# A hybrid model on one Trainium2 core: the first block's order of work laid out anew, four of its units' segments on GpSimd, and the first expert unit's gate and up inside it

## The chip, the cores and the metric

One core of a Trainium2 chip runs the whole kernel. The core has five engines that run in parallel, each with its own queue of instructions taken strictly in order: TensorE (matmul, PE in the profile), VectorE (DVE), ScalarE (ACT), GpSimd (POOL) and SyncE (SP, which here issues the DMAs). They wait for each other through semaphores. TensorE writes only to PSUM, eight banks of 128 x 512 f32; SBUF is the large on-chip memory. The metric is device time in microseconds, the median of several runs.

## The reference, cut to what matters

The input is x of 4 sequences x 512 tokens x 128 features in f32. Four layers follow, each added to its own input after a layer norm:

```python
x = x + attn_a(layernorm(x))   # rotary q, then a Mamba-2 style scan
x = x + ffn(layernorm(x))      # 8 experts, the best 2 per token, and a shared one
x = x + attn_b(layernorm(x))   # RWKV time mixing and channel mixing
x = x + ffn(layernorm(x))      # the same expert layer again
```

In attn_a, q is projected and rotated, normed (rmsnorm) and projected to z (256), xBC (512) and dt (4 heads). xBC passes a causal convolution of four taps and silu. dt = softplus. The scan runs in chunks: within a chunk y = (C B^T * L) (x dt), where L = exp of the segment sums of dt*A; between chunks a state of 128 x 64 per head is decayed and added to. y + D x is multiplied by silu(z), normed and projected by W_out to 128 features, and q is added.

In ffn each branch is (silu(x Wg) * (x Wu)) Wd with 256 hidden features; the result is weighted by the router.

## The kernel before, in words

The program has two blocks, `phase_mamba` (layer 1) and `phase_body` (layers 2 to 4). A block ends when all engines have reached its end; then the next begins. In both, every engine's order of work is written out by hand.

**First block.** A tile is 128 tokens; there are 16, four per sequence. The block first norms x (VectorE `statistics`, `normalise`), turns it (`turn_x`), projects q (`project_q`), multiplies by the rotary tables (`turn_q`, `add_q`), norms and turns again (`turn_h`), and projects: `project_in` for the convolution (16 banks of 512 columns; VectorE adds three taps each in `taps`, ScalarE does the first, `tap0`), `project_z` (L1060: one tile of 256 columns in one bank, ScalarE `z_silu`, 16 times) and `project_dt`. dt passes exp and ln on ScalarE (`dt_exp`, `dt_log`) and becomes adt in `finish_dt`; until then no segment can be made. `turn_tok` turns the convolved tokens back.

The scan then works in 16 units, each one tile of one sequence: units 0 to 7 belong to sequences 0 and 1, units 8 to 15 to sequences 2 and 3. Per unit n: ScalarE `segments` (L807) writes `seg_l[n % 2]` as four products of 128 x 128; TensorE `seg_sums` (L1097) sums them, ScalarE `seg_exp` takes the exponential; TensorE `products` makes C B^T, VectorE `masking` and `mixing` join the two; GpSimd `weigh_x`, `skip_x` and `decay_x` prepare x dt, D x and the weighted x; TensorE `within` and `carry` make y, `add_state` the state, VectorE `joining` and `new_state` read them; GpSimd `gating` multiplies by silu(z); then comes the way out: TensorE `turn_g`, ScalarE `copy_gT`, TensorE `project_out`, and VectorE `closing` adds q. All ways out use one bank, so `turn_g(n)` waits for `closing(n - 1)` (L1150). Beside it, `split_high` and `split_low` cut the nine branches' expert weights into two f16 halves each.

At the end of the block `tile_stats`, `tile_means` (L593) and GpSimd's `rsqrt_out` (L344) make the layer norm of the expert layer, the first half of the tiles and the second; `apply_norm`, `turn_first`, `copy_x`, `cast_x` and `split_x` prepare the first sequence's input to the experts (x_hi and x_lo).

**Second block.** 72 units, one branch of one sequence (slot q, branch e, u = 9q + e). Per unit and half: TensorE `gate_up` (L1533) makes gate and up, three f16 matmuls of 512 columns each; ScalarE `gate` takes silu; VectorE `hidden` multiplies; ScalarE `high` casts; GpSimd `low` makes the rest; two units later TensorE's `down` (L1550) follows. The router's `logits` stand beside unit 0, with the exponential in `route_exp` on ScalarE. `beside` places the work of layer 3 between units. The statistics of sequence 3 are made in slot 1 (`has_stats`, L1522); those of the first three sequences come from the first block.

## Time and profile before

| | |
|---|---|
| median of 3 runs | 508.76 us (507.75 to 509.42) |
| the profiled execution | 507.94 us, of which 505.6 us span |
| TensorE busy | 470.4 us, 93% of the span |
| VectorE, ScalarE, GpSimd busy | 391.0, 360.3 and 360.6 us |
| mean granted TensorE clock | 0.982 |
| first block | from 0 to about 133 us |

The page of the profile has these lines:

```profile
PE   3787999998599999999999999999999989999994
DVE  5897999777376687889888898888887868477664
ACT  1789999874375867976696958694886566868552
POOL 4564676788276658789879879888889586466652
PEclk9999899999599999999999999999999999999999
```

Each digit is the busy share of a fortieth of the span (12.6 us) in tenths, and PEclk is TensorE's granted clock in tenths of full speed. The eleventh slice, 126 to 139 us, is the end of the first block and the start of the second: all four engines have a low digit there, and the clock stands at 5. A granted clock of 1.00 is 2.4 GHz and 0.50 is 1.2 GHz. Busy time of matmuls overlaps from one to the next.

### The profile page before, as it was taken

Reading aid. Unit: us, or ns where it says so; the run is one execution under the profiler, and the core shown is the slowest. Engines: PE = TensorE matmul, PEld = TensorE weight load, DVE = VectorE, ACT = ScalarE, POOL = GpSimd, SP = SyncE. Lnnn points to the kernel's source line nnn. Section 1 sums busy time; section 2 is a strip of 40 time slices with the busy share of each in tenths; the row PEclk is TensorE's granted clock in tenths of the full one; section 3 lists DMA queues with packets and bytes.
Section 4 is the critical chain, followed back from the end, with each engine's and each line's share of the span. In section 5 each row is a group of like instructions: output and inputs, shape, how many; then the busy total and the mean of one; then the engine's idle time right before and its main releaser. Section 6 shows DMA issues by size and latency. Waiting matters only on the chain.

```text
span 505.6 us, 10587 instructions
## 1 busy us (share of the span) xinstructions
PE 470.4 (93%) x3662; PEld 322.8 (64%) x3662; DVE 391.0 (77%) x1051; ACT 360.3 (71%) x711; POOL 360.6 (71%) x445
## 2 busy tenths in 40 slices
PE   3787999998599999999999999999999989999994
PEld 2555788997256666665565765666566756666663
DVE  5897999777376687889888898888887868477664
ACT  1789999874375867976696958694886566868552
POOL 4564676788276658789879879888889586466652
PEclk9999899999599999999999999999999999999999
DMA  8102011000010000000000000000000000000000
GB/s 275 38 3 87 8 32 33 1 2 3 6 63 0 2 1 2 2 2 1 1 2 1 1 1 1 1 2 3 0 1 22 2 1 23 0 2 1 22 1 21
DMA packets 7012, 8.49 MB, mean 17 GB/s; under 512 B 560, under 2 KB 5168, under 8 KB 6960
## 3 DMA queue, kind: packets, MB, share of 16 engines
q1 hardware_dynamic: 6960, 7.83, 4.8%
q8 instruction: 29, 0.48, 0.4%
q14 instruction: 23, 0.19, 0.1%
HBM read 6.78 MB, written 1.05 MB: 15 GB/s over the span
## 4 chain that ended last, share of the span: by engine, by line
PE 55%; DVE 8%; POOL 5%; ACT 3%; issue 2%; DVEq 0%; POOLq 0%; ACTq 0%
PE bank L1544 9%; PE bank L1548 9%; PE bank L1545 9%; PE bank L1563 5%; PE bank L1565 5%; PE bank L1564 5%; PE bank L1680 3%; PE bank L1663 2%; PE bank L1606 2%; DVE x L1914 2%; PE bank L1607 2%; POOL b_hc L2195 1%; PE bank L1591 1%; PE bank L1570 1%; DVE b_hid L1898 1%
## 5 line engine op out<-in xcount | busy, mean ns | idle before, releaser
L2133 POOL TENSOR_TENSOR b_hid_lo<-b_hid,b_hid_hi 128x512 f16<-128x512 f32 x144 | 167.8, 1177 | 56.7 <-ACT b_hid_hi L1740 54.5
L1898 DVE SCALAR_TENSOR_TENSOR b_hid<-bank,b_silu 128x512 f32<-128x512 f32 x144 | 97.8, 688 | 62.0 <-ACT b_silu L1733 36.7
L1733 ACT ACTIVATE b_silu<-bank 128x512 f32<-128x512 f32 x144 | 85.9, 597 | 58.9 <-PE bank L1548 58.5
L1544 PE MATMUL bank<-x_hi,wsplit 128*128 128x512 f16 x288 | 110.2, 382 | 5.5 <-PEq L130 4.8
L1545 PE MATMUL bank<-x_hi,wsplit 128*128 128x512 f16 x288 | 110.2, 382 | 0.0
L1548 PE MATMUL bank<-x_lo,wsplit 128*128 128x512 f16 x288 | 110.2, 382 | 0.0
L1563 PE MATMUL bank<-wsplit,b_hid_hi 128*128 128x128 f16 x576 | 100.2, 219 | 4.3 <-DVE x L1914 2.6
L1740 ACT CAST b_hid_hi<-b_hid 128x512 f16<-128x512 f32 x144 | 88.2, 612 | 21.9 <-DVE b_hid L1898 21.7
L1565 PE MATMUL bank<-wsplit,b_hid_lo 128*128 128x128 f16 x576 | 100.2, 219 | 0.0
L1564 PE MATMUL bank<-wsplit,b_hid_hi 128*128 128x128 f16 x576 | 100.2, 219 | 0.0
L1914 DVE SCALAR_TENSOR_TENSOR x<-bank,b_w_branch,x 128x128 f32<-128x128 f32 x256 | 71.5, 342 | 16.1 <-PE bank L1565 16.0
L1563 PEld LDWEIGHTS bank<-wsplit,b_hid_hi 128*128 128x128 f16 x576 | 56.6, 98 | 15.1 <-POOL b_hid_lo L2133 5.6
L1564 PEld LDWEIGHTS bank<-wsplit,b_hid_hi 128*128 128x128 f16 x576 | 56.3, 98 | 7.1 <-issue 1.3
L1565 PEld LDWEIGHTS bank<-wsplit,b_hid_lo 128*128 128x128 f16 x576 | 56.4, 98 | 0.0
L1548 PEld LDWEIGHTS bank<-x_lo,wsplit 128*128 128x128 f16 x288 | 28.4, 99 | 34.7 <-issue 1.1
L1544 PEld LDWEIGHTS bank<-x_hi,wsplit 128*128 128x128 f16 x288 | 28.4, 99 | 33.9 <-issue 8.8
L1545 PEld LDWEIGHTS bank<-x_hi,wsplit 128*128 128x128 f16 x288 | 28.3, 98 | 27.6 <-issue 4.8
L502 DVE SCALAR_TENSOR_TENSOR xbc<-bank,cols,xbc 128x511 f32<-128x511 f32 (+2 forms) x48 | 35.6, 747 | 2.0 <-ACT xbc L775 0.7
L812 ACT ACTIVATE seg_l<-after,adt 128x128 f32<-128x128 f32 x64 | 20.4, 401 | 0.0
L1106 PE MATMUL bank<-causal,seg_l 128*128 128x128 f32 x128 | 17.9, 285 | 0.0
L334 POOL TENSOR_TENSOR g<-y,sz 128x256 f32<-128x256 f32 x16 | 12.6, 787 | 7.4 <-DVE y L577 5.9
L1106 PEld LDWEIGHTS bank<-causal,seg_l 128*128 128x128 f32 x128 | 16.8, 200 | 1.2 <-issue 0.8
(237 smaller groups left out, 932.6 us busy)
## 6 DMA issues: line engine op xcount, KB each, us to landing
moe_raw<-in_moe SPq DMA_DIRECT2D x9, 384.0 KB, 4.6
x<-in_x SPq DMA_DIRECT2D x4, 256.0 KB, 3.9
out<-x SPq DMA_DIRECT2D x4, 256.0 KB, 2.3
rope<-in_rope SPq DMA_DIRECT2D x1, 512.0 KB, 6.0
wzx<-in_wzx SPq DMA_DIRECT2D x1, 386.0 KB, 6.4
b_w_rkvo<-in_w_rkvo SPq DMA_DIRECT2D x1, 256.0 KB, 2.6
b_w_fk<-in_w_fk SPq DMA_DIRECT2D x1, 256.0 KB, 2.8
b_w_fv<-in_w_fv SPq DMA_DIRECT2D x1, 256.0 KB, 3.6
```

Of the source, the lines that this page charges most:

```text
L502: ins = nc.vector.scalar_tensor_tensor(xbc[:, b, t0 + back:t1], conv_ps[b % 2][:, 0:SEQ - back], col(core, "conv_w", TAPS * b + TAPS - 1 - ...
L1544: nc.tensor.matmul(dst, hi, x_hi[:, q % 2, :], start=True, stop=False)
L1545: nc.tensor.matmul(dst, lo, x_hi[:, q % 2, :], start=False, stop=False)
L1548: nc.tensor.matmul(dst, hi, x_lo[:, q % 2, :], start=False, stop=True).then_inc(made, 1)
L1563: nc.tensor.matmul(dst, h_hi, d_hi, start=blk == 0, stop=False)
L1564: nc.tensor.matmul(dst, h_hi, d_lo, start=False, stop=False)
L1565: ins = nc.tensor.matmul(dst, h_lo, d_hi, start=False, stop=blk == FBLK - 1)
L1733: nc.scalar.activation(silu[:, 2 * (u % 2) + blk, :], gate_ps[blk][:, :], ACT.Silu, scale=GU_UNSCALE).then_inc(silu_ready, 1)
L1740: nc.scalar.copy(hid_hi[:, FBLK * (u % 3) + blk, :], hid[:, 2 * (u % 2) + blk, :]).then_inc(hi_ready, 1)
L1898: nc.vector.scalar_tensor_tensor(hid[:, 2 * (u % 2) + blk, :], up_ps[blk][:, :], GU_UNSCALE * H_SCALE, silu[:, 2 * (u % 2) + blk, :], ALU. ...
L1914: ins = nc.vector.scalar_tensor_tensor(x[:, i, :], down_ps[:, P * c:P * (c + 1)], w_branch[:, q % 2, e, c:c + 1], x[:, i, :], ALU.mult, AL ...
L2133: nc.gpsimd.tensor_tensor(hid_lo[:, slot, :], hid[:, 2 * (u % 2) + blk, :], hid_hi[:, slot, :], ALU.subtract).then_inc(lo_ready, 1)
```

## The change

- **Segments.** Units 1, 3, 5 and 7 (`SEG_POOL`) get their segments from GpSimd, one product of 128 x 512 with broadcast operands (`segments_here`); the others stay on ScalarE. They have a semaphore of their own, `segp_ready`.
- **Banks.** q, hT, conv, z, y and the way out move to other banks. In units 8 to 15 segments and y have two banks each, as before. The way out gets a second bank: from unit 11 on odd units use bank 7, and `turn_g(n)` then waits for `closing(n - 2)`.
- **z** comes two tiles at a time, eight times, into a whole bank.
- **Warm-up.** 22 matmuls of the identity by itself stand in front of TensorE's first `turn_x`.
- **The second half's layer norm** leaves the first block: `tile_stats` 8 to 15, the second `tile_means` and the second `rsqrt_out` go, and the second block makes the statistics of sequences 2 and 3 in slots 0 and 1.
- **First expert unit.** `first_unit(0)` and `first_unit(1)` make unit 0's gate and up inside the first block, in banks 0, 2 and 1, 3; `gate_up(0, ...)` is skipped in the second. The semaphores `gate_made` and `up_made` live across the two blocks.
- **silu's table** is loaded at the end of the first block (`load_silu`), and the dummy silu at the start of the second is gone.
- **Order.** All four engines' lists of the first block are written anew; with the exception of what is named above they hold the same steps.

```diff
+    SECOND_OUT = 11
+    SEG_POOL = (1, 3, 5, 7)
...
-        xnT_ps, q_ps, hT_ps, conv_ps, z_ps, tok_ps = (
-            core.banks[0], core.banks[1:3], core.banks[3], core.banks[4:6], core.banks[6], core.banks[7])
-        dt_ps, cum_ps, cb_ps, out_ps, st_ps, turn_ps = (
-            core.banks[2], core.banks[3], core.banks[2], core.banks[3], core.banks[6], core.banks[7])
+        banks = core.banks
+        xnT_ps, q_ps, hT_ps, conv_ps, z_ps, tok_ps = banks[0], (banks[4], banks[2]), banks[6], (banks[1], banks[5]), banks[3], banks[7]
+        dt_ps, cum_ps, cb_ps, st_ps, turn_ps = banks[2], banks[6], banks[2], banks[3], banks[7]
...
+        def out_ps(n):
+            return banks[7 if n >= SECOND_OUT and n % 2 else 6]
...
+            def segments_here(n):
+                pool.wait_ge(dt_step, ADT)
+                if n >= 2:
+                    pool.wait_ge(seg_made, n - 1)
+                nc.gpsimd.tensor_tensor(seg_l[:, n % 2], core.after[:].unsqueeze(1).broadcast_to([P, HEADS, P]),
+                                        adt[:, tile_of(n), :].unsqueeze(2).broadcast_to([P, HEADS, P]),
+                                        ALU.mult).then_inc(segp_ready, 1)
...
-            def z_silu(i):
-                act.wait_ge(z_made, i + 1)
-                nc.scalar.activation(sz[:, i, :], z_ps[:, 0:INNER], ACT.Silu).then_inc(z_done, 1)
+            def z_silu(k):
+                act.wait_ge(z_made, k + 1)
+                nc.scalar.activation(sz[:, 2 * k:2 * k + 2, :].rearrange("p c d -> p (c d)"), z_ps[:, :],
+                                     ACT.Silu).then_inc(z_done, 1)
...
+            def load_silu():
+                nc.scalar.activation(sq_junk[:, 0:1], core.ident[:, 0:1], ACT.Silu)
...
             def turn_g(n):
                 pe.wait_ge(g_ready, n + 1)
-                if n:
+                if n == 0:
+                    pe.wait_ge(dt_act, DECAYS)
+                elif n == SECOND_OUT:
+                    pe.wait_ge(first_ready, 1)
+                elif n > SECOND_OUT:
+                    pe.wait_ge(x_ready, n - 1)
+                else:
                     pe.wait_ge(x_ready, n)
...
+            def warm_up(count):
+                for _ in range(count):
+                    nc.tensor.matmul(tok_ps[:, 0:P], core.ident[:], core.ident[:], start=True, stop=True)
+
+            def first_unit(blk):
+                pe.wait_ge(first_ready, 2)
+                pe.wait_ge(moe_lo, 1)
...
+                pe.wait_ge(normed, TPS + 1)
+                for part, bank, made in ((0, banks[blk], core.gate_made), (2, banks[2 + blk], core.up_made)):
+                    hi = core.wsplit[:, 0, part, P * blk:P * (blk + 1)]
+                    lo = core.wsplit[:, 0, part + 1, P * blk:P * (blk + 1)]
+                    nc.tensor.matmul(bank[:, :], hi, shared.x_hi[:, 0, :], start=True, stop=False)
+                    nc.tensor.matmul(bank[:, :], lo, shared.x_hi[:, 0, :], start=False, stop=False)
+                    nc.tensor.matmul(bank[:, :], hi, shared.x_lo[:, 0, :], start=False, stop=True).then_inc(made, 1)
```

Around these the lists change. The end of three of them, before and after:

```diff
 TensorE
             turn_g(12)
-            within(14)
+            turn_g(13)
             project_out(12)
             within(15)
-            turn_g(13)
             project_out(13)
             turn_g(14)
+            first_unit(0)
             project_out(14)
-            turn_first()
             turn_g(15)
             project_out(15)
+            first_unit(1)
 VectorE
-            apply_norm()
             closing(14)
             split_low(7)
-            split_low(8)
             closing(15)
-            tile_stats(14)
-            tile_stats(15)
-            split_x()
-            tile_means(1)
+            split_low(8)
 ScalarE
             copy_gT(15)
-            copy_x()
-            cast_x()
+            load_silu()
```

`turn_first`, `apply_norm`, `copy_x`, `cast_x` and `split_x` stand earlier in the new lists, around units 10 to 12.

In the middle, between `project_dt(3)` and the first segments, TensorE's list was `project_z(11)`, `project_in(2, 0)`, `turn_tok(3)`, `project_in(2, 1)`, `turn_tok(4)`, `products(0)`, `cumulate()` and is now `project_in(2, 1)`, `turn_tok(3)`, `project_z(6)`, `turn_tok(4)`, `project_in(2, 2)`, `products(0)`, `cumulate()`. On VectorE `taps(2, 0)` and two low splits stand before `finish_dt()`, where three low splits stood. GpSimd's list now begins its unit work with `skip_x(0)`, the residuals, `weigh_x(0)`, `weigh_x(1)`, `segments_here(1)`; `segments_here(3)` stands behind `decay_x(2)`, `segments_here(5)` behind `weigh_x(4)` and in front of `gating(1)`, `segments_here(7)` behind `decay_x(5)`.

## Rows read from the trace of the kernel before

**Rows 1.** Windows: busy time (instructions) of each engine, granted clock, DMA share, GB/s.

```profile
50.00:60.00 10.00, 9.54 (x55) 8.09 (x55) 9.12 (x17) 9.97 (x26) 4.64 (x8) 0.83 0.07 27
70.00:80.00 10.00, 10.00 (x70) 8.66 (x70) 9.72 (x22) 9.34 (x25) 6.13 (x11) 1.00 0.01 2
150.00:200.00 50.00, 49.99 (x463) 32.47 (x461) 35.91 (x112) 33.38 (x61) 34.70 (x37) 1.00 0.01 1
```

**Rows 2.** Waits of TensorE, 7 to 60 us: total us, times, longest.

```profile
PE bank L1094 <- DVE adt L521: 1.6, 1, 1.6
PE bank L1065 <- ACT sz L781: 1.2, 2, 0.8
```

**Rows 3.** Waits of TensorE, 68 to 122 us, all of them.

```profile
PE bank L1165 <- ACT gT L834: 0.4, 1, 0.4
```

**Rows 4.** Timeline of the join: start, us, engine, line, operation, count, idle before.

```profile
127.46 1.22 PE L1165 MATMUL bank<-w_gated,gT 128*128 128x128 f32 x4 [0.46 <-ACT gT L834]
...
130.96 1.65 POOL L1393 TENSOR_TENSOR ln_moe_rstd<-ln_moe_veps,mhalf 128x8 f32<-128x8 f32 x1 [5.21 <-DVE ln_moe_veps L599]
...
132.97 0.20 POOL L1395 TENSOR_SCALAR ln_moe_nbias<-ln_moe_nbias 128x8 f32<-128x8 f32 x1
...
133.53 0.59 PE L1544 MATMUL bank<-x_hi,wsplit 128*128 128x512 f16 x1 [4.85 <-PEq L130]
```

**Rows 5.** Windows with the granted clock, around dt and behind the join.

```profile
50.00:54.00 4.00, 4.00 (x20) 3.82 (x21) 3.54 (x7) 3.98 (x11) 1.87 (x4) 0.57 0.17 67
...
133.50:139.00 5.50, 5.47 (x15) 2.33 (x15) 0.78 (x2) 3.49 (x6) 1.03 (x16) 0.50 0.11 14
```

**Rows 6.** Timeline, up to the start of unit 2's gate.

```profile
140.34 0.23 ACT L1799 ACTIVATE b_ex<-b_shift 128x32 f32<-128x32 f32 x1 [0.37 <-DVE b_shift L1935]
...
140.68 1.28 ACT L1733 ACT_TABLE_LOAD   x1
...
142.62 0.39 PE L1544 MATMUL bank<-x_hi,wsplit 128*128 128x512 f16 x1 [0.17 <-ACT b_silu L1733]
```

**Rows 7.** Timeline of the tail, from within(15) on.

```profile
121.13 1.00 PE L1137 MATMUL bank<-xdt,mix 128*128 128x64 f32 x8
...
121.39 0.33 DVE L586 SCALAR_TENSOR_TENSOR x<-bank,rms,q 128x128 f32<-128x128 f32 x1
...
123.12 0.72 POOL L334 TENSOR_TENSOR g<-y,sz 128x256 f32<-128x256 f32 x1
...
125.54 1.03 PE L1173 MATMUL bank<-ident,norm 128*128 128x128 f32 x4
...
126.08 1.82 DVE L531 SCALAR_TENSOR_TENSOR wsplit<-moe_raw,wsplit 128x768 f16<-128x768 f32 x2
```

**Rows 8.** The page's costliest groups: busy us, mean ns of one, idle before, releaser.

```profile
L1898 DVE SCALAR_TENSOR_TENSOR b_hid<-bank,b_silu 128x512 f32<-128x512 f32 x144 | 97.8, 688 | 62.0 <-ACT b_silu L1733 36.7
L1733 ACT ACTIVATE b_silu<-bank 128x512 f32<-128x512 f32 x144 | 85.9, 597 | 58.9 <-PE bank L1548 58.5
L1544 PE MATMUL bank<-x_hi,wsplit 128*128 128x512 f16 x288 | 110.2, 382 | 5.5 <-PEq L130 4.8
```

**Rows 9.** Groups of the first block, 0 to 134 us.

```profile
L812 ACT ACTIVATE seg_l<-after,adt 128x128 f32<-128x128 f32 x64 | 20.4, 401 | 0.0
...
L293 POOL TENSOR_TENSOR q<-q,x 128x512 f32<-128x512 f32 x4 | 5.0, 1276 | 0.0
...
L591 DVE BATCH_NORM_STATS2 ln_moe_stats<-x 128x6 f32<-128x128 f32 x16 | 3.9, 278 | 0.0
```

**Rows 10.** Timeline of the start: the first sixteen projections of q.

```profile
9.35 3.72 PE L1026 MATMUL bank<-wq,normT 128*128 128x256 f32 x8 [0.77 <-ACT normT L758]
...
15.61 1.99 PE L1026 MATMUL bank<-wq,normT 128*128 128x256 f32 x8
```

**Rows 11.** The tile mix, 50 to 125 us: ns min/median/max, first and last start.

```profile
L545 DVE TENSOR_TENSOR mix<-expo,gm x16: 678/689/1237, 55.5 to 119.0; 128x512 f32<-128x512 f32 x16
```

**Rows 12.** Waits of all engines, 68 to 90 us: GpSimd's longest for TensorE.

```profile
POOL xdt L316 <- PE bank L1137: 3.2, 2, 2.6
```

More of the change, by code:

```diff
@@ L371, in _ @@
             add_residuals(2)
-            skip_x(0)
+            add_residuals(3)
+            weigh_x(0)
+            weigh_x(1)
+            segments_here(1)
             skip_x(1)
-            gate_w_out(1)
-            weigh_x(0)
-            add_residuals(3)
+            weigh_x(2)
             decay_x(0)
-            weigh_x(1)
-            gating(0)
             decay_x(1)
             decay_x(2)
-            weigh_x(2)
-            weigh_x(3)
+            segments_here(3)
+            gating(0)
@@ L384, in _ @@
             skip_x(2)
             skip_x(3)
+            skip_x(4)
+            decay_x(3)
+            skip_x(5)
             rms_g(0)
+            weigh_x(3)
             weigh_x(4)
+            segments_here(5)
             gating(1)
+            gating(2)
             weigh_x(5)
-            decay_x(3)
-            skip_x(4)
-            decay_x(4)
-            skip_x(5)
             weigh_x(6)
             skip_x(6)
+            rms_g(1)
+            decay_x(4)
+            gating(3)
             decay_x(5)
-            rms_g(1)
+            segments_here(7)
@@ L443, in _ @@
-            skip_x(15)
             gating(13)
@@ L944, in _ @@
+            copy_gT(1)
+            square_g(1)
+            tok_out(8)
+            square_g(2)
+            tap0(3, 2)
+            tok_out(9)
+            segments(6)
+            seg_exp(5)
+            split_high(4)
+            split_high(5)
             tap0(3, 3)
-            seg_exp(5)
-            segments(7)
-            split_high(5)
-            square_g(2)
+            copy_gT(2)
             seg_exp(6)
-            copy_gT(2)
+            square_g(3)
+            tok_out(10)
             segments(8)
-            tok_out(9)
@@ L1283, in _ @@
             turn_tok(12)
-            project_out(3)
+            project_out(4)
             within(6)
-            turn_g(4)
+            products(8)
+            turn_g(5)
             add_state(8)
             turn_tok(13)
-            project_out(4)
-            seg_sums(9)
-            turn_g(5)
+            project_out(5)
+            within(7)
+            turn_tok(14)
+            carry(7)
             products(9)
-            within(7)
-            carry(7)
+            turn_g(6)
             seg_sums(10)
-            project_out(5)
@@ L1316, in _ @@
+            add_state(9)
+            carry(10)
+            turn_tok(15)
+            project_out(7)
+            within(10)
+            add_state(10)
+            turn_g(8)
+            products(12)
+            seg_sums(11)
+            project_out(8)
             add_state(11)
             seg_sums(12)
-            project_out(8)
-            carry(12)
-            carry(13)
-            seg_sums(13)
-            add_state(12)
-            turn_tok(15)
-            turn_g(9)
-            within(12)
@@ L1326, in _ @@
-            project_out(9)
-            within(13)
-            turn_g(10)
-            products(14)
-            add_state(13)
+            turn_g(9)
+            carry(11)
+            products(13)
+            within(11)
+            seg_sums(13)
+            carry(12)
+            project_out(9)
+            within(12)
+            seg_sums(14)
+            turn_first()
+            turn_g(10)
+            add_state(12)
+            products(14)
+            products(15)
+            carry(13)
@@ L1331, in _ @@
+            turn_g(11)
             project_out(10)
-            seg_sums(14)
-            turn_g(11)
-            seg_sums(15)
-            products(15)
             project_out(11)
             carry(14)
+            add_state(13)
+            within(13)
+            within(14)
+            seg_sums(15)
             carry(15)
             turn_g(12)
-            within(14)
+            turn_g(13)
             project_out(12)
             within(15)
-            turn_g(13)
             project_out(13)
```

542 lines of the change are left out of this document (258 added, 284 removed).

## The prediction, made before the changed kernel had run

> **What bounds the kernel now.** I read the windows table first, then TensorE's waits, then the timeline around the join of the two blocks. The expert block is TensorE's: in 150 to 200 us it is busy 49.99 of 50 us [rows 1]. The first block has three parts. Up to about 68 us TensorE still waits for others (1.6 us for dt before 50 us, 1.2 us for z's bank [rows 2]) while ScalarE is full (9.97 of 10 us in 50 to 60 [rows 1]). From 68 to 122 us TensorE's waits come to 0.4 us in all [rows 3], so there only less work, or work done sooner, moves the end. From 122 us a tail of single round trips follows and then the join. What the first block costs after 122 us is plain time: nothing of the expert block can lie beside it.
>
> The join is where most of it is lost. The last output projection ends at 127.46 + 1.22 = 128.68 us. TensorE's next matmul starts at 133.53 us, because VectorE still makes the means of the second half and GpSimd its pow (130.96 + 1.65) and two more steps, up to 132.97 + 0.20 = 133.17 us; only then does the next block start, 0.36 us later [rows 4]. TensorE then runs at 0.50 of its clock [rows 5], so the first twelve expert matmuls come at half speed, and unit 2's gate starts only at 142.62 us, behind exp, a table load and a silu on ScalarE [rows 6]. From the last projection to unit 2's gate it is 142.62 - 128.68 = 13.94 us.
>
> **The change, step by step.** Call E the end of the last output projection.
>
> 1. *Join.* The statistics of tiles 8 to 15, their means and the second rsqrt_out leave the first block. Behind E are left: on VectorE closing(15) and split_low(8), 0.33 us as an earlier closing and 0.91 us as each of two low splits [rows 7]; on TensorE the six matmuls of first_unit(1), 1.3 us at full clock (half of the 0.43 us at which they came at half clock; the page's 382 ns of one overlaps its neighbours [rows 8]), at most 6 x 0.38 = 2.3. ScalarE's silu table load stands behind copy_gT(15), which is before E. So the block ends at E + 1.4 and the next starts at E + 1.4 + 0.36 = E + 1.8 (at most E + 2.7). There ScalarE does silu, silu (2 x 0.60), waits for VectorE's first product (0.60 + 0.69 = 1.3) [rows 8] and casts it (I take the silu's 0.60): 1.9; the exp table takes 1.28 (as long as the one for silu [rows 6]): 3.2; from the start of that exp to unit 2's gate it was 142.62 - 140.34 = 2.3 [rows 6]. Unit 2's gate starts at E + 1.8 + 5.5 = E + 7.3. Before: E + 13.9. **-6.6 us.** TensorE's own work in between (logits 1.25 us or less, unit 1's twelve matmuls 2.6) is done at E + 5.7 and hidden by ScalarE's table loads. Should ScalarE be later by x, the gain is smaller by x.
> The moved statistics: four bn_stats of 278 ns [rows 9] with means and one GpSimd rsqrt in unit 6 and 8 of the first slot. The slot has VectorE at 35.91 of 50 us [rows 1]; I take 0, and 1.5 us if TensorE had no slack for them.
>
> 2. *Clock at the join.* TensorE had waited 1.6 us for dt just before 50 us [rows 2], and then ran at 0.50 for most of 50 to 54 us (mean 0.57) [rows 5]. Now it waits about 1.6 us (E + 5.7 to E + 7.3), after shorter ones. I take the same again: some 3.4 us at half rate (0.43 of 4 us lost = 1.7 us). **+1.6 us**; bounds 0 (no fall) and 2.8 (half of the 5.5 us at 0.50 after 133.5 us [rows 5]).
>
> 3. *Tail.* Before, within(15) ends at 121.13 + 1.00 = 122.13 us and E is 128.68: 6.55 us, since every turn_g waits for the closing before it (one bank), and turn_first (1.03 us at the falling clock) stands in between [rows 7]. Now odd units use bank 7, so turn_g(15) waits for g(15) alone: g ends 123.12 + 0.72 = 123.84, that is 1.7 us after within(15) [rows 7]; turning 0.4, copy 0.37, projection 0.7 and the hops between make 2.0. So 3.7 instead of 6.55, **-2.8 us**; turn_first moves to where TensorE is full, 0.5 us, **net -2.3**. first_unit(0), 1.3 us, stands in the idle of that chain (the other work there is two projections and a turn, 1.2 us, of 3.7) and costs nothing; without that cover it costs 1.3.
>
> 4. *Before 122 us.* ScalarE loses four units of segments: each is four activations of 401 ns [rows 9], at most 1.6 us a unit and some 1.3 where they overlap, so 5 to 6 us, and z comes in eight activations instead of sixteen. GpSimd gets four products of 128x512, 1.28 us each by its own row for that size [rows 9]: 5.1 us, into 30 us of which it was busy about 60% (4.64 and 6.13 of 10 [rows 1]). TensorE's work is the same. It gains only what it idled: in the dt wait now stand conv and z matmuls (1.0 of 1.6 us [rows 2]), with that the half clock of 50 to 54 us goes (1.7 [rows 5]), and z takes eight round trips, not sixteen (0.5 of 1.2 [rows 2]). **-3.2 us.** What then comes late is VectorE, busy 9.1 and 9.7 of 10 us there [rows 1]. Bounds: 0, and -5.5 if all of these waits and the half clock go (1.6 + 1.2 + 1.7) and a further 1.0 of shorter gaps with them.
> The warm-up: 22 f32 matmuls before the first turn_x. The first eight projections of q took 3.72 us, the next eight 1.99 [rows 10]: 1.7 us to win; but from about 2.3 us on 44 passes run past 7.4 us, when turn_x(0) is ready, and delay it by 1 to 2 us. I take 0, bounds -1 and +1.
> Swapped banks otherwise: z, conv, q and st have the same number as before; 0.
>
> Rule weighed: on GpSimd products run beside VectorE's mixing. The trace has mixing at 689 ns median and 1237 at most [rows 11]. The Trainium skill, GPSIMD Engine Reference, 1. Specifications, says that GpSimd shares its SBUF interfaces with VectorE, with contention when a VectorE instruction has two SBUF inputs, as mixing has; the trace agrees. By the rows each of the four new products can lengthen one mixing by up to 0.55 us: at most 2.2 us of VectorE. I leave it inside the bound of step 4, as most mixings stay at 689.
> Another rule speaks against step 1. In the trace the exp table's follow-up is seamless: w_decay's exp is over when the 1.28 us load starts at 140.68, and unit 2's gate comes 1.94 us after that start [rows 6]. The Trainium skill, ScalarE: Activation LUTs, What ACT_TABLE_LOAD costs, adds 1.38 us of drain to every switch; with one more such drain in the chain the estimate by that page would be 1.4 us less gain, 499.4. The row decides.
>
> **Sum.** -6.6 + 1.6 - 2.3 - 3.2 = -10.5 us on the profiled execution's 507.94: 497.4. The median of the runs, 508.76, is 0.8 above that execution; I forecast **498.0**, between 497.4 and 498.3.
>
> **Rivals.**
> A. *The middle gives nothing:* TensorE waits in program order behind VectorE, which stays full; only join, clock and tail count. -6.6 + 1.6 - 2.3 = -7.3: 501. For it: 0.4 us of waits in 54 us [rows 3], VectorE at 9.7. Against: the wait for dt and the half clock are TensorE's own.
> B. *No fall of the clock at the join, and the whole bound in the middle:* -6.6 - 2.3 - 5.5 = -14.4: 494. For it: first_unit keeps TensorE busy through the tail, where before it idled (waits in three round trips) and fell.
> C. *Slower: the segments on GpSimd become TensorE's wait.* seg_sums(1, 3, 5, 7) stand in TensorE's order in front of everything else; segments_here(5) stands behind gating(0) and weigh_x(4), themselves behind products of TensorE. If each comes late by its own 1.28 us and by a wait as long as GpSimd's longest there for TensorE (2.6 us, xdt [rows 12]), that is 4 x 3.9 = 15.6 us against -7.3: +8.3, 516. It decides from 1.8 us of lateness per unit (7.3 / 4). Against: two seg buffers, and dt is all that each needs.
>
> **Numbers.** Forecast 0.55, A 0.22, B 0.15, C 0.04, anything else 0.04. Its own range is 495.5 to 500.5; with A and B inside: 492.8 to 503.5. A measurement of this kernel tells 0.3% (1.5 us) from no change. Faster by more 0.92, the same 0.03, slower 0.05.
>
> **What would show it.** Join: the gap between the last output projection and the first logits near 1.8 us, no ScalarE table load in front of the first silu, unit 2's gate 7.3 us after the projection. Clock: one stretch at 0.50 near unit 2, none near 50 us. Tail: within(15) to last projection 3.7 us. Middle: last projection near 123 us (128.68 - 2.3 - 3.2). GpSimd's segments at 1.3 us. Wrong if TensorE waits for seg_l, if it idles inside the tail for mixing(15), or if the expert block itself gets longer by the moved statistics.

## The result, and the profile after

The changed kernel takes 496.58 us, the median of four runs (495.72 to 498.08). The kernel before, over four runs, takes 508.25 us. The ratio is 0.9769, with a 95% interval of 0.9744 to 0.9795: faster by 11.7 us. The profiled execution of after took 496.6 us (span 494.9, mean granted clock 1.000) against 507.94 (505.6, 0.982) before. The forecast was 498.0 us.

In the page of the profile after, each digit is a fortieth of the span (12.4 us) in tenths. TensorE's busy share and its clock:

```profile
PE   7898999999899999999999999999999989999994
...
PEclk9999999999999999999999999999999999999999
```

TensorE's busy time, 470.8 us, is what it was (470.4 before), in a span that is 10.7 us shorter. The hole at the join (5 in the eleventh slice of before, with the clock at 5) is an 8, and PEclk has no low digit left. What went is idle time and time at half clock, not work.

The timeline of after around the join shows it. Columns: start, duration, engine, line, operation, count, and in brackets the idle before it with what ended it.

```profile
123.86 1.28 ACT L853 ACT_TABLE_LOAD   x1
123.89 0.71 PE L1177 MATMUL bank<-w_gated,gT 128*128 128x128 f32 x4 [0.46 <-ACT gT L843]
...
126.22 1.08 ACT L1762 ACTIVATE b_silu<-bank 128x512 f32<-128x512 f32 x2 [0.86 <-PEq L135]
126.25 1.03 PE L1618 MATMUL bank<-router_w,normT_moe 128*128 128x8 f32 x8 [0.34 <-PEq L135]
...
128.21 1.28 ACT L1828 ACT_TABLE_LOAD   x1
129.51 0.23 ACT L1828 ACTIVATE b_ex<-b_shift 128x32 f32<-128x32 f32 x1
129.85 1.28 ACT L1762 ACT_TABLE_LOAD   x1
131.14 0.60 ACT L1762 ACTIVATE b_silu<-bank 128x512 f32<-128x512 f32 x1
131.79 0.39 PE L1571 MATMUL bank<-x_hi,wsplit 128*128 128x512 f16 x1 [1.91 <-ACT b_silu L1762]
```

The last output projection ends at 123.89 + 0.71 = 124.60 us. Silu's table loads beside it. `first_unit(1)` fills TensorE to 125.90 us, and 0.34 us later the next block is running. The first silu comes 1.62 us and the first logits 1.65 us after the projection; unit 2's gate starts at 131.79, that is 7.19 us after it, where before it was 13.94 [rows 4, 6].

Timeline of TensorE and GpSimd in the tail, from `within(15)` on:

```profile
119.76 1.00 PE L1145 MATMUL bank<-xdt,mix 128*128 128x64 f32 x8
...
121.75 0.73 POOL L341 TENSOR_TENSOR g<-y,sz 128x256 f32<-128x256 f32 x1 [0.42 <-DVE y L595]
...
123.05 0.38 PE L1169 MATMUL bank<-ident,g 128*128 128x128 f32 x2
```

`within(15)` ends at 120.76 us; g is ready at 122.48. `turn_g(15)`'s matmuls show no idle in front of them: the six matmuls of `first_unit(0)` run up to 122.77 us, `project_out(14)` follows, and `turn_g(15)` comes 0.57 us after its g is ready. 124.60 - 120.76 = 3.84 us, where it was 6.55 [rows 7].

Windows of both kernels over the middle; columns: stretch and its length, busy us (instructions) of PE, PEld, DVE, ACT and POOL, granted clock, DMA share, GB/s. Before, beyond [rows 1]:

```profile
27.00:50.00 23.00, 18.80 (x94) 12.21 (x93) 19.26 (x30) 21.50 (x48) 11.62 (x19) 1.00 0.13 41
...
100.00:110.00 10.00, 10.00 (x77) 9.54 (x76) 7.16 (x24) 8.43 (x26) 8.83 (x16) 1.00 0.01 2
110.00:120.00 10.00, 10.00 (x78) 9.27 (x76) 8.69 (x28) 5.96 (x20) 8.14 (x14) 1.00 0.01 2
```

And after:

```profile
27.00:50.00 23.00, 20.67 (x107) 14.22 (x106) 21.04 (x34) 22.03 (x46) 13.23 (x22) 1.00 0.05 14
50.00:60.00 10.00, 9.41 (x68) 7.91 (x68) 8.93 (x16) 9.74 (x19) 8.89 (x13) 1.00 0.17 50
...
100.00:110.00 10.00, 9.58 (x74) 8.90 (x73) 7.28 (x18) 7.26 (x23) 8.94 (x15) 1.00 0.01 2
110.00:120.00 10.00, 9.38 (x64) 8.11 (x63) 9.19 (x20) 5.06 (x15) 6.00 (x9) 1.00 0.01 2
```

Here the gain is small. The half clock after dt is gone (0.83 in 50 to 60 us before, 1.00 now), and TensorE is busy for 1.9 us more between 27 and 50 us. This is work moved forward: from the first eight projections of q to adt the trace has 22 matmuls of `project_in` and 28 of `project_z`, where before had 20 and 24, and behind adt so many fewer. By the start-to-start times of these matmuls (0.43 and 0.22 us) that is an estimated 1.7 us. But it now has 1.0 us of idle between 100 and 120 us, where it had none. The waits of TensorE in after, up to 60 us and from there to 122 us (total us, times, longest), name 0.8 us of it, behind `gm` and x:

```profile
PE bank L1077 <- ACT xtok L799: 1.3, 3, 0.8
PE bank L1098 <- DVE adt L539: 1.0, 1, 1.0
...
PE bank L1098 <- DVE gm L556: 0.5, 1, 0.5
PE bank L1169 <- DVE x L604: 0.3, 1, 0.3
```

Milestones of the two profiled executions, with starts and ends taken from the timelines:

| | before | after | difference |
|---|---|---|---|
| adt ready | 49.70 | 49.14 | -0.56 |
| `within(15)` ends | 122.13 | 120.76 | -1.37 |
| last output projection ends | 128.68 | 124.60 | -4.08 |
| unit 2's gate starts | 142.62 | 131.79 | -10.83 |
| unit 9's gate starts | 170.71 | 159.88 | -10.83 |
| unit 71's gate starts | 491.98 | 481.26 | -10.72 |

The profiled execution's time fell by 11.3 us, 10.7 in the span and 0.6 around it. So the change is over once unit 2 begins: from unit 9 to unit 71 it is 321.3 and 321.4 us, with the statistics of sequences 2 and 3 in slots 0 and 1.

### The profile page after: what moved, and what is told of

Its sections match the earlier page's. It is cut to its first block, busy times and chain, and to the rows that moved or that the text cites. A ratio compares the mean times of both kernels' runs of the same rounds, so it can differ in the third digit from the quotient of the medians.

```text
span 494.9 us, 10643 instructions
## 1 busy us (share of the span) xinstructions
PE 470.8 (95%) x3706; PEld 325.5 (66%) x3706; DVE 389.5 (79%) x1043; ACT 355.9 (72%) x687; POOL 366.7 (74%) x449
## 4 chain that ended last, share of the span: by engine, by line
PE 55%; DVE 9%; POOL 5%; ACT 3%; issue 2%; DVEq 0%; POOLq 0%; ACTq 0%
PE bank L1571 9%; PE bank L1575 9%; PE bank L1572 9%; PE bank L1590 5%; PE bank L1592 5%; PE bank L1591 5%; PE bank L1707 3%; PE bank L1690 2%; PE bank L1633 2%; DVE x L1941 2%; PE bank L1634 2%; POOL b_hc L2222 1%; PE bank L1597 1%; DVE b_hid L1925 1%; PE bank L1618 1%
## 5 line engine op out<-in xcount | busy, mean ns | idle before, releaser
L1571 PE MATMUL bank<-x_hi,wsplit 128*128 128x512 f16 x284 | 107.7, 379 | 2.4 <-ACT b_silu L1762 1.9
L1575 PE MATMUL bank<-x_lo,wsplit 128*128 128x512 f16 x284 | 107.6, 379 | 0.0
L1572 PE MATMUL bank<-x_hi,wsplit 128*128 128x512 f16 x284 | 107.6, 379 | 0.0
L1571 PEld LDWEIGHTS bank<-x_hi,wsplit 128*128 128x128 f16 x284 | 27.9, 98 | 29.7 <-issue 2.9
L1572 PEld LDWEIGHTS bank<-x_hi,wsplit 128*128 128x128 f16 x284 | 27.8, 98 | 26.7 <-issue 4.0
L1145 PEld LDWEIGHTS bank<-xdt,mix 128*128 128x128 f32 x128 | 16.4, 192 | 0.7
```

Of the source, the lines that this page charges most:

```text
L1571: nc.tensor.matmul(dst, hi, x_hi[:, q % 2, :], start=True, stop=False)
L1572: nc.tensor.matmul(dst, lo, x_hi[:, q % 2, :], start=False, stop=False)
L1575: nc.tensor.matmul(dst, hi, x_lo[:, q % 2, :], start=False, stop=True).then_inc(made, 1)
```

## The experiments

"Changed kernel" is after. Every kernel was timed beside the kernel before on one chip, and ratios are to those times. To compare with after, its ratio of 0.9769 is used, and a second measurement of after itself:

**c1_changed_again.** The changed kernel once more, with no edit, on the chip of e8, n2 and n3 below.

> The changed kernel itself beside the others of this chip, for the size of n1 to n3 and for the spread of its executions. Expected: median 496.6, and among six executions one or two 1.5 to 1.7 us above the rest, in which the clock stood at 0.50 for some 3.4 us behind the join (as in one of the four so far, 498.08 at a mean clock of 0.995). Rival: no such second group.

Measured: 496.73 us (495.76 to 498.05), ratio 0.9767 [0.9747, 0.9787], as at first. Its profiled execution was its slowest, 498.05, and shows where the slowest runs differ from the rest: of the eight of both measurements, the two at 498.05 and 498.08 have a mean clock of 0.995, the six others (495.72 to 496.78) 0.999 or 1.000. These are its windows behind the join, and then the one of after's own profile that answers to the second:

```profile
131.00:133.00 2.00, 1.49 (x6) 0.57 (x7) 1.20 (x2) 2.00 (x5) 0.96 (x1) 0.92 0.82 263
133.00:135.00 2.00, 2.00 (x6) 0.71 (x5) 1.83 (x9) 1.25 (x3) 2.00 (x3) 0.50 0.51 165
135.00:137.00 2.00, 2.00 (x23) 1.45 (x22) 0.75 (x2) 0.82 (x2) 1.53 (x2) 0.72 0.00 0
```

```profile
133.00:135.00 2.00, 2.00 (x17) 1.15 (x16) 1.83 (x9) 1.76 (x4) 2.00 (x3) 1.00 0.54 174
```

In both, TensorE waited 1.9 us for silu ahead of unit 2. In one execution the clock then fell to 0.50 and in the other it did not, with the same program. From unit 2's gate to unit 9's it is 29.78 us with the fall (131.50 to 161.28) and 28.09 without: 1.69 us. That is the +1.6 of step 2, but as something that comes in some executions. Differences of 1 us between two kernels of this list may be nothing but this.

**e7_before_stats.** The kernel before with one part of the change: the second half's statistics go to the second block.

```diff
-            rsqrt_out(1)
...
-            tile_stats(8)
-            tile_stats(9)
...
-            tile_stats(14)
-            tile_stats(15)
...
-            tile_means(1)
...
-            return q >= SEQS - 1
+            return q >= 2
```

> The kernel before with one part of the change alone: the second half's statistics leave the first block and are made in slots 0 and 1. Theory 1: the block ends behind split_x, about 1.5 us after the last projection instead of 4.5: -3.1 us, and the half clock of 126 to 139 us stays: 505. Rival 2: the clock does not fall so long, 503 or less. Rival 3: the statistics in the second block cost what they save: 508.

Measured: 504.38 us (504.14 to 504.52), ratio 0.9911 [0.9891, 0.9931]: -4.5 us by the ratio (-4.8 by the medians). In its timeline the new block's first matmul comes 1.44 us after the last projection, and from the projection (129.69) to unit 2's gate (139.13) it is 9.44 us instead of 13.94. The clock still falls, for a shorter time:

```profile
132.00:136.00 4.00, 4.00 (x16) 1.98 (x14) 1.01 (x2) 2.77 (x6) 0.52 (x2) 0.58 0.01 2
```

**e5_stats_back.** The reverse: the changed kernel with the statistics back in the first block.

```diff
-            rsqrt_out()
+            rsqrt_out(0)
...
+            rsqrt_out(1)
...
+            tile_stats(14)
+            tile_stats(15)
+            tile_means(1)
...
-            return q >= 2
+            return q >= SEQS - 1
```

> The changed kernel with the second half's statistics, means and rsqrt in the first block again (tile_stats 8 to 15, tile_means(1), rsqrt_out(1)); the second block makes only sequence 3's, as before. Theory 1 (my step 1): the block ended 4.49 us after the last projection before and 1.3 after; +3.2 us there: 499.8, or 502 if the clock falls in the longer gap. Rival 2: it is not the statistics but the order of VectorE's list that shortened the join: within 0.5 us of 496.6.

Measured: 501.45 us (500.20 to 502.48), ratio 0.9853 [0.9827, 0.9878]: +4.3 us by the ratios. The pow and the first silu behind it, in its timeline:

```profile
128.29 1.65 POOL L1432 TENSOR_TENSOR ln_moe_rstd<-ln_moe_veps,mhalf 128x8 f32<-128x8 f32 x1 [2.93 <-DVE ln_moe_veps L618]
```

The last projection ended at 125.65, the first silu starts at 130.85 (5.2 us later, not 1.62), and unit 2's gate at 137.36 (11.71 instead of 7.19: +4.5). Of these 4.5 us, 3.6 are there at the first silu; the other 0.9 come while the clock stands at 0.50, from 131.17 to 138.00 us. Taken alone in the old kernel and taken away from the new one, this part is worth nearly the same (4.5 and 4.3 us). It is the largest single part of the change.

**e4_no_first.** Unit 0's gate and up back in the second block.

```diff
-            first_unit(0)
...
-            first_unit(1)
...
-                    if u:
-                        gate_up(u, 0)
+                    gate_up(u, 0)
```

> The changed kernel with unit 0's gate and up in the second block again (gate_up(0) as in the kernel before). Theory 1: the block still ends about 1.3 us after the last projection, as VectorE's closing and low split need that long; then silu waits for three and nine matmuls: unit 2's gate comes 1.3 to 1.5 us later, the clock stays at 1.00: 498.0. Rival 2: first_unit is what keeps TensorE busy enough; without it the clock falls at the join and the time is 499.5 to 501. Rival 3: nothing, since ScalarE's two table loads hide it all: 496.6.

Measured: 499.41 us (499.25 to 499.57), ratio 0.9824 [0.9803, 0.9845]: +2.8 us. Last projection 123.95, unit 2's gate 134.53: 10.58 us instead of 7.19. TensorE waits 2.05 us at the join with nothing to do, and the window right after it shows the clock at half:

```profile
127.00:129.00 2.00, 2.00 (x6) 0.73 (x5) 0.37 (x1) 0.60 (x1) 0.00 (x0) 0.50 0.00 0
```

From the end of `within(15)` (120.56) to the last projection (123.95) it is 3.39 us without `first_unit(0)`, 3.84 with it: of its 1.3 us the round trip hides some 0.85, and 0.45 show, where step 3 had counted nothing. The 3.4 us of the join are two things: the first silu comes 3.32 us after the projection instead of 1.62, and the other 1.7 us come behind it, where TensorE has unit 0 still to do and stands at half clock from 126.25 to 129.66 us.

**e6_no_load.** silu's table is not loaded at the end of the first block; the dummy silu at the start of the second is back.

```diff
-            load_silu()
...
+            nc.scalar.activation(silu[:, 0, 0:1], core.ident[:, 0:1], ACT.Silu).then_inc(act_step, 1)
+            act.wait_ge(act_step, 1)
```

> The changed kernel without load_silu at the end of the first block; the second begins with the dummy silu and its table load again, as before. Theory 1: in the join ScalarE's chain to unit 2's gate is what TensorE waits for (1.91 us), so 1.28 + 0.2 us are added to it: 498.1. Rival 2: hidden behind logits and unit 1's gate and up on TensorE: 496.6.

Measured: 498.87 us (497.64 to 499.91), ratio 0.9802 [0.9775, 0.9829]: 1.7 us more by the ratios, with intervals that overlap. ScalarE's timeline shows what stands in front:

```profile
126.06 1.28 ACT L1898 ACT_TABLE_LOAD   x1 [2.36 <-PEq L135]
...
127.59 1.08 ACT L1761 ACTIVATE b_silu<-bank 128x512 f32<-128x512 f32 x2
```

From the last projection (124.46) to unit 2's gate (133.16) it is 8.70 us, 1.5 more than in after: the load and the dummy (0.20 us), whole.

**e3_one_out.** The way out has one bank in all units; three steps are moved so that the lists fit it.

```diff
-    SECOND_OUT = 11
+    SECOND_OUT = 99
...
+            closing(10)
...
-            closing(10)
...
-            turn_g(13)
...
             within(15)
+            turn_g(13)
```

> The changed kernel with one bank for the way out of all units (turn_g(n) waits for closing(n-1) again; turn_g(11), turn_g(13) and closing(10) moved by one to three places in their lists, without which it would stand still). Theory 1 (my step 3): the tail from within(15) to the last output projection goes from 3.84 us back towards 6.55: +2.0 to +2.7, 498.6 to 499.3. Rival 2: the second bank adds nothing, the tail is short because turn_first and the two rsqrt steps have left it: 496.6.

Measured: 503.39 us (502.93 to 503.80), ratio 0.9901 [0.9884, 0.9919]: +6.7 us by the ratios, more than twice what was expected. Its waits of TensorE from 100 to 132 us, and its windows in the tail:

```profile
PE bank L1169 <- DVE x L604: 3.9, 4, 1.9
PE bank L1177 <- ACT gT L843: 1.8, 4, 0.5
```

```profile
120.00:131.00 11.00, 7.17 (x36) 4.74 (x34) 4.76 (x8) 3.59 (x12) 4.09 (x9) 0.84 0.00 1
```

From `within(15)` (122.64) to the last projection (131.89) it is 9.25 us, not 3.84 and not before's 6.55. That is 5.4 us of the whole; another 1.7 us come between adt and `within(15)` (73.28 us for 71.61), where the way out of units 11 to 14 has one bank too. With one bank, every `turn_g` waits for the closing before it, and `turn_g(13)` had to go behind `within(15)`. `first_unit(0)` is then no filler but stands in that chain: it starts at 126.51 us, the clock falls to 0.50 at 127.00, its last four matmuls end 0.57 to 0.63 us after their start instead of 0.38, and `project_out(14)`, whose input is there at 127.08, starts at 128.59. So the second bank and the early expert unit belong together in this order. That the early unit is why the tail is longer than before's is read from this timeline; one bank without it was not tried.

**e2_seg_act.** All segments on ScalarE, those of units 1, 3, 5 and 7 put right behind those of units 0, 2, 4 and 6.

```diff
-    SEG_POOL = (1, 3, 5, 7)
+    SEG_POOL = ()
...
-            segments_here(1)
...
+            segments(1)
```

> The changed kernel with all sixteen units' segments on ScalarE (units 1, 3, 5, 7 right behind 0, 2, 4, 6 in its list); GpSimd has none. ScalarE gets 4 x 1.28 = 5.1 us back into 50 to 90 us, where it is busy 9.6 to 9.9 of 10. Theory 1: the middle of the block gained 1.9 us, most of it by this relief: 498.5. Rival 2: TensorE's order is the bound there and ScalarE has slack: 496.6. Rival 3: ScalarE is the bound of the whole stretch, and all 5.1 us come back: 501.7.

Measured: 502.67 us (500.12 to 502.86), ratio 0.9880 [0.9858, 0.9902]: +5.6 us. Its profiled execution is an outlier, at 500.12 us and a mean clock of 0.999, 3.5 us above after's; the five others take 502.34 to 502.86 at 0.995 to 0.997. So the trace holds 3.5 us; the some 2 us more of the others go with a lower mean clock, and no trace of them was kept. In the profiled one adt comes at 48.50, but from there to the end of `within(15)` it takes 75.88 us instead of 71.61: +4.3. ScalarE is full and TensorE idles by 2.2 of 10 us:

```profile
50.00:60.00 10.00, 7.82 (x54) 6.32 (x55) 6.88 (x13) 9.97 (x23) 5.71 (x10) 1.00 0.10 33
```

**e8_before_segpool.** The kernel before with the same four segments on GpSimd, in its old lists: `segments_here(1)` to `(7)` among GpSimd's steps, `segments(1)` to `(7)` gone from ScalarE's.

```diff
+    SEG_POOL = (1, 3, 5, 7)
...
+            segments_here(1)
...
-            segments(1)
```

> The kernel before with one part of the change alone: segments of units 1, 3, 5 and 7 on GpSimd, 5.1 us less for ScalarE, in lists that are otherwise the old ones (GpSimd's four products behind skip_x(0), decay_x(2), weigh_x(4), decay_x(5)). Taking the same thing away from the changed kernel cost 5 to 6 us. Theory 1: the worth lies in the order of work that was written for it; in the old lists TensorE is never kept waiting after 68 us, so 0 to 1.5 us, 506.5 to 508. Rival 2: it is worth the same in both: 503.

Measured: 511.13 us (509.83 to 513.72), ratio 1.0055 [1.0033, 1.0078]: slower by 2.8 us by the ratio. adt comes at 51.16; from there to `within(15)` it takes 74.76 us, where before took 72.43. Waits of all engines from 60 to 100 us, and a window of the same stretch:

```profile
POOL seg_l L353 <- PE bank L1119: 3.8, 2, 2.1
...
PE bank L1150 <- DVE mix L558: 1.5, 1, 1.5
```

```profile
80.00:90.00 10.00, 8.07 (x62) 7.25 (x62) 8.83 (x18) 6.79 (x17) 8.59 (x15) 1.00 0.11 35
```

GpSimd stands with a segment until TensorE has read the buffer, 3.8 us in all, and its other products (xdt, g) stand behind it in its list; TensorE is busy only 8.07 of 10 us, where ScalarE has now room (6.79). This is the mechanism that rival C feared, and its sign is right: in these two kernels the move off ScalarE gains only where GpSimd's place for it comes after the buffer is free. In the changed kernel the same product costs

```profile
50.43 1.04 POOL L359 TENSOR_TENSOR seg_l<-after,adt 128x512 f32<-128x512 f32 x1
```

and the four of them have no idle before them. The segments' move alone is -5.6 us in the new order (-3.5 in the traces) and +2.8 in the old, each for the one placing that was tried; another place for the products in either list might give another number.

**e1_no_warm.** The 22 matmuls of the identity at the start are left out.

```diff
-            warm_up(22)
```

> The changed kernel without the 22 warm-up matmuls. In its trace they end at 9.69 us, so the first turn_x starts at 9.53 us instead of 7.43 before the change; in return the sixteen first projections of q run at full rate (1.97 us for eight against 3.72). Theory 1 (my step 4): both cancel, 496.6 within 1 us, though the first projections take about 3.7 us for eight again. Rival 2: the warm-up costs more than it gives, since 7.4 us of it stand in front of the chain that starts the block: 495.4 or less. Rival 3: it is what keeps the clock up until 50 us: without it the half clock near 50 us comes back and the time is 498.5.

Measured: 497.45 us (496.70 to 500.61), ratio 0.9795 [0.9769, 0.9822]; not to be told from after. Its timeline at the start, and then after's:

```profile
7.42 1.15 PE L1018 MATMUL bank<-ident,norm 128*128 128x128 f32 x4 [7.42 <-DVE norm L494]
9.34 3.75 PE L1027 MATMUL bank<-wq,normT 128*128 128x256 f32 x8 [0.77 <-ACT normT L766]
```

```profile
2.27 7.42 PE L1183 MATMUL bank<-ident 128*128 128x128 f32 x44 [2.27 <-POOL after L265]
9.53 0.60 PE L1018 MATMUL bank<-ident,norm 128*128 128x128 f32 x4
10.89 1.97 PE L1027 MATMUL bank<-wq,normT 128*128 128x256 f32 x8 [0.77 <-ACT normT L766]
```

With the warm-up the first turn takes 0.60 us and the first eight projections of q 1.97, both at full clock; without it 1.15 and 3.75, at half. But the warm-up is not over until 9.69 us, and the first turn starts at 9.53 instead of 7.42. So the projections end at 12.86 and 13.09 us: what the clock gives, the wait takes. No half clock stands near 50 us in this kernel either, so the one of before [rows 5] did not go because of the warm-up. The three traces with the old lists (before, e7, e8) all have such a fall, from 50.46, 53.45 and 53.11 us on; of the eleven with the new lists none has it.

The next three kernels use these findings.

**n1_late_route.** The router of slot 0 moves two units later, so that neither of ScalarE's two table loads stands between unit 0's silu and unit 2's gate.

```diff
-                if (e, place) == (0, 3):
+                if (e, place) == ((2 if q == 0 else 0), 3):
...
-                if (u, place) == (1, 0):
+                if (u, place) == (3, 0):
...
-                if (e, place) == (1, 0):
+                if (e, place) == ((3 if q == 0 else 1), 0):
...
-                if (e, place) == (1, 2):
+                if (e, place) == ((3 if q == 0 else 1), 2):
```

> The changed kernel with the router's exponential of slot 0 moved from unit 0 to unit 2 on ScalarE (w_decay's with it, so the two table loads too), and VectorE's second part of the routing two units later. Theory 1: the 1.91 us for which TensorE waits for ScalarE in front of unit 2's gate go, since from unit 2 on the downs lie beside: 494.7. Rival 2: the table loads only move, and TensorE waits as long in front of unit 4: 496.6. Rival 3: without the wait the clock never falls there, and the executions lie closer together, 494.5 to 495.

Measured: 495.47 us (494.88 to 495.60), ratio 0.9734 [0.9717, 0.9751]. Unit 2's gate comes 5.12 us after the last projection and has no wait in front of it; from the projection to unit 9's gate it is 33.81 us instead of 35.28. From unit 2's gate to unit 9's it is 28.69 us where after had 28.09, so of the 2.07 us won at unit 2's gate 0.6 go again to the steps that moved. The four runs lie within 0.72 us, those of after within 2.4, and their mean clocks are 0.998 and 0.999: no sign of a fall behind the join. Four runs are few: n2 below, which has no such wait either, spreads by 1.55 us, with its slowest run at a mean clock of 0.995 and no trace of it.

**n2_late_warm14.** n1 with 14 identity matmuls instead of 22.

```diff
-            warm_up(22)
+            warm_up(14)
```

> The faster version n1 (late router exponential) with 14 warm-up matmuls for 22. With 22 the first turn_x started at 8.9 to 10.1 us though its input is ready at 7.4. Theory 1: 28 passes end at 7.5 to 8.3 us, the first chain starts 1 to 1.5 us sooner, and since ScalarE and VectorE are full from 20 us on about 1 us arrives: 494.4. Rival 2: too few to raise the clock before the projections of q: as without warm-up, 496.

Measured: 493.98 us (493.27 to 494.82), ratio 0.9712 [0.9694, 0.9729], the best version of all: 2.9 us under after by the ratios, and 2.8 under c1 on the same chip. Under n1 it is 1.1 us by the ratios, with intervals that overlap, and 1.6 under n3 on the same chip, where no two runs overlap. Its start:

```profile
2.27 4.97 PE L1183 MATMUL bank<-ident 128*128 128x128 f32 x28 [2.27 <-POOL after L265]
7.10 1.10 PE L1018 MATMUL bank<-ident,norm 128*128 128x128 f32 x4
8.96 1.97 PE L1027 MATMUL bank<-wq,normT 128*128 128x256 f32 x8 [0.77 <-ACT normT L766]
```

The clock rose inside the warm-up: its passes start 0.21 us apart up to 5.6 us and 0.11 us apart from there. The first turn is not delayed (7.10 us); its 1.10 us are VectorE's pace, whose four norms start 0.26 us apart from 6.69 us on, as the turn's four matmuls do. The projections run at full clock, up to 10.93 us instead of 12.86. Those 1.9 us are kept: adt is ready at 47.24, not 49.14, and the last projection ends at 122.69.

**n3_late_warm8.** n1 with 8 of them.

```diff
-            warm_up(22)
+            warm_up(8)
```

> n1 with 8 warm-up matmuls. They end before 6 us. Theory 1: the clock has then not risen when the first turn_x comes, the first eight projections take 3 us or more, and the time is that of n1 or 0.5 more: 495.5 to 496. Rival 2: any early activity does: 494.4 as with 14.

Measured: 495.62 us (495.14 to 496.56), ratio 0.9746 [0.9728, 0.9764]. Its timeline has the eight projections slow again:

```profile
10.10 3.75 PE L1027 MATMUL bank<-wq,normT 128*128 128x256 f32 x8 [0.77 <-ACT normT L766]
```

So with eight the projections came at half clock as without any, but not because the clock had not risen, as theory 1 has it. The passes are 0.11 us apart from 5.2 us on; then TensorE idles for 2.38 us, and the clock falls to 0.50 at 8.61, in the midst of the first turn:

```profile
2.27 3.43 PE L1183 MATMUL bank<-ident 128*128 128x128 f32 x16 [2.27 <-POOL after L265]
8.09 1.25 PE L1018 MATMUL bank<-ident,norm 128*128 128x128 f32 x4 [2.38 <-DVE norm L494]
```

With 22 the first turn is delayed, and with 14 neither happened. The first turn of n3's execution stood behind x's norm until 8.09 us, those of n2 and e1 started at 7.10 and 7.42: x's norm is ready up to 1 us earlier or later from run to run. So the 1.9 us of n2's profile hold some of this; the timed runs give 1.1 us over n1, and how a later norm would do with 14 was not seen.

## Why the forecast held, step by step

**1. Join, -6.6: right.** Measured -6.75 (13.94 to 7.19). Both halves of the working hold: block start 1.6 us after the projection (1.8 said), then 5.6 us (5.5 said) of ScalarE's chain with exp's and silu's tables, which ends last. The wait of 1.91 us at unit 2's gate is the one that step 2 named (1.6). The single parts add up to more than the whole: undone singly, the statistics are worth 4.5 us of this stretch, `first_unit` 3.4 and silu's table 1.5, together 9.4 against 6.75. The first two of these each hold a stretch at half clock (e5, e4) that after's own execution does not have, so the sum counts it twice. The moved statistics cost nothing in the slots: 321.3 and 321.4 us from unit 9 to unit 71.

In after's rows exp starts 0.02 us after its 1.28 us load ends (129.49 to 129.51), and silu's load starts at 129.85, 0.02 us after `w_decay`'s exp, the last one, ends at 129.83. The Trainium skill, ScalarE: Activation LUTs, What ACT_TABLE_LOAD costs, adds 1.38 us of drain to each switch; no row here shows it, and e6_no_load moved the join by 1.5 us, one load and one dummy.

**2. Clock, +1.6: right in size, wrong in kind.** I took the fall as certain. It happens in some executions: not in after's profiled one, but in c1's, where it cost 1.69 us, and in that of e1_no_warm. The profiled execution therefore lacks the term. Its mechanism (a wait in front of unit 2's gate) fits n1, in which the wait is gone and no mean clock of four runs shows the fall.

**3. Tail, -2.8: right.** Measured -2.71 (6.55 to 3.84), of which `first_unit(0)` takes 0.45 (e4), so the round trip itself, 3.39 us, is shorter than worked out (3.7). e3_one_out shows that the second bank is needed for it: without it the tail is 5.4 us longer in the new order, not 2.7, the place of `turn_g(13)` and a half clock included. That `turn_first` costs about 0.5 us where TensorE is full was not tried by itself.

**4. Before 122 us, -3.2: too large.** With `turn_first`'s +0.5 the step gave -2.7 for the end of `within(15)`; measured is -1.37. It is this term that was mis-sized, by 1.3 us, and with it the last projection comes at 124.60 us, not near 123. Up to adt I counted 1.0 for the dt wait and 0.5 for z, 1.5 in all; 0.56 came. The step took TensorE's idle for time won. From the first projections of q to adt TensorE idles 6.84 us before (36.63 less 29.79 busy) and 4.33 after (36.28 less 31.95), 2.5 us less; but that was filled with 2.2 us more of busy time, much of it the matmuls moved forward, and adt comes hardly sooner. The dt wait went from 1.6 to 1.0 us, z's wait of 1.2 [rows 2] is gone whole, but TensorE now waits 1.3 us for `xtok` where ScalarE is full. Before, that wait was 0.5 us, by the same view of the kernel before from 7 to 60 us:

```profile
PE bank L1073 <- ACT xtok L790: 0.5, 1, 0.5
```

So part of the wait changed its name. From adt to `within(15)` the half clock should have given 1.7 less 0.5 for `turn_first`, so 1.2; 0.82 came (72.43 to 71.61). With the estimated 1.7 us of matmuls that had left this stretch, it should have been 2.9. TensorE's idle in it rose instead, from 1.13 us (72.43 less 71.30 busy) to 1.86 (71.62 less 69.76). The waits that the trace names are 1.2 us, new ones for `gm` (0.5), x (0.3), `seg_l` (0.2, for a segment of ScalarE's, not of GpSimd's) and `expo` (0.2), against 1.0 before: 0.4 [rows 3] and, ahead of the 68 us at which those rows begin,

```profile
PE bank L1157 <- POOL g L334: 0.6, 1, 0.6
```

So the named waits account for 0.2 of the 2.1 us that are missing, and the idle for 0.7. I had called TensorE's work the same and named VectorE as what comes late next, with no price on it. Where the rest went is open, and whether `gm` is late through VectorE's order or through the bank of `products` was not tried.

*Segments.* The forecast priced them at 1.28 us each on GpSimd; they take 1.04. It did not see how much hangs on them: it counted them inside a step of -3.2, while e2_seg_act shows that the new order without them, with the segments placed as there, stands 5.6 us worse. The order was laid out for them: by these runs it costs without them and gains with them.

The rule weighed there speaks of contention. The 16 mixings of after take 674, 689 and 1101 ns (minimum, median, maximum), in the kernel before 678, 689 and 1237 [rows 11]. Mixings with nothing of GpSimd's beside them take 678 to 693 ns in both traces; the long ones, four before (899 to 1237) and four after (990 to 1101), each have one of its products of 128 x 256 beside them (xdt, dx, xw or g), though not every such neighbour makes one long. Of the four new products one alone stood beside a mixing, for 0.17 us, and that one took 720 ns. The Trainium skill, GPSIMD Engine Reference, 1. Specifications, has the contention; these long mixings agree with it, but the new products have no visible share in it.

*Warm-up, 0: right*, as the balance said: the projections end 0.2 us earlier, and e1 can't be told from after. n2 shows that the balance could be won, by 1.1 us against n1.

**The sum.** Profiled execution: -6.75 - 2.71 - 1.37 = -10.83, and 0.11 us given back in the body; forecast -6.6 + 1.6 - 2.3 - 3.2 = -10.5. That the sum came so near is in part luck. Two errors cancelled: the clock, too dear by 1.6 in this execution, and the middle, too good by 1.3. The median of 496.58 lies between the forecast and rival B (494), and half of B is right (the clock does not always fall). Its other half, a large gain in the middle, is wrong. Rival A (501) gives the middle nothing, +0.5 with `turn_first`; the measured -1.37 lies between that and the forecast's -2.7, nearer to the forecast. Rival C (516) did not come, but e8 shows its mechanism alive in the old lists.

## What to carry to other kernels

Read the join of two program stages as its own stage: here 9.5 of 10.8 us of the gain (6.75 + 2.71) lay behind the last scan unit's `within`, where the engines stood in each other's round trips, and the cheapest cure was to move work that only a later consumer needs behind the barrier. Price an engine swap together with the order around it: the same four products moved from ScalarE to GpSimd were worth -5.6 us in lists made for them and +2.8 in lists that were not. When a wait goes, look at which engine was full beside it: here part of TensorE's wait came back as a wait for ScalarE. And an idle engine's time is won only if what it then does sooner is what the end waits for: TensorE idled 2.5 us less ahead of adt, and adt came 0.56 us sooner. And where one kernel's runs spread by more than its neighbours', look for a short wait behind which the clock may fall: removing the wait of 1.9 us (n1) gained 1.5 us in the trace, and its four runs lay closer together.

## What the runs showed of the hardware that was not expected

- The granted clock is not a function of the program: after the same wait of 1.9 us in front of unit 2's gate it stayed at 1.00 in one execution of the changed kernel and fell to 0.50, for some 3.4 us, in another. Price: 1.69 us.
- Waking the clock ahead of the first real work paid here only where it ended about when that work was ready. With 44 f32 passes of the identity (7.42 us) and with 28 (4.97 us) the first projections of q took 1.97 us, with 16 (3.43 us) and with none 3.75. In the run with 16 the clock had risen at 5.2 us and fell again at 8.61, behind 2.38 us of idle.
- The clock rose at different times behind the same matmuls: with 44 passes begun at 2.27 us, at 7.0 us in after's profile and at 8.05 in n1's.
- GpSimd's product of 128 x 512 with both operands broadcast took 1.04 us, that with two full operands 1.28 us in the kernel before [rows 9].
